# A routed layer of 64 experts at the end of an audio tower: eight rounds of eight experts become one written-out sequence

## The reference, cut to what matters

```
scores = sigmoid(x2 @ gate_w.T)                  # 5520 x 64; top 4 of 8 groups, then top 8 experts
xb = zeros(E, CAP, DIM).at[flat_e, pos].set(x_rep, mode='drop')     # E = 64, CAP = 256, DIM = 128
h  = silu(einsum('ecd,edm->ecm', xb, w1)) * einsum('ecd,edm->ecm', xb, w3)   # 64 hidden columns
yb = einsum('ecm,emd->ecd', h, w2)
y  = yb.at[flat_e, pos].get(mode='fill', fill_value=0.0) * w.reshape(-1)[:, None]
out = h3 + y.reshape(T, K, DIM).sum(1)           # h3 is the stream of 5520 rows before this part
```

## Time and profile before

| | |
|---|---|
| median of 3 runs | 2299.24 us (2298.69 to 2302.49) |
| profiled execution, its own time | 2305.26 us |
| its span in the profile | 2303.4 us |
| busy share of PE, DVE, ACT, POOL over the span | 85%, 63%, 37%, 32% |
| last scatter issued, first add issued, last add issued | 2030.12, 2043.60, 2279.72 us |
| closing DMA issued, end of span | 2283.61, 2303.4 us |

### The profile page before, as it was taken

One profiled execution on the slowest core, in us unless ns is written; L12 is line 12 of the kernel. 1 busy time (PEld: TensorE's weight loads), 2 busy tenths in 40 slices (PEclk: granted clock), 3 DMA queues, 4 the chain that ended last, 5 costly groups with the idle time before them and its releaser, 6 DMA issues. The chain is left out here.

```text
span 2303.4 us, 46715 instructions
## 1 busy us (share of the span) xinstructions
PE 1959.6 (85%) x16960; PEld 1579.7 (69%) x16960; DVE 1457.8 (63%) x4386; ACT 863.2 (37%) x2193; POOL 741.2 (32%) x630
## 2 busy tenths in 40 slices
PE   3688999999999999999999999999988887266660
PEld 2677887888788788878887888788776565133440
DVE  4784465677677766776676766666666668344440
ACT  2453454444344434443434443434334341021120
POOL 1000000013132322323232323232325235768885
PEclk9999999999999999999999999999999899577775
DMA  6874744434344333423342424133200001057665
GB/s 213 277 265 135 252 160 146 144 121 130 93 125 126 111 105 109 124 86 115 94 129 68 121 83 127 50 117 93 80 2 10 6 4 25 8 108 126 115 92 72
DMA packets 167588, 251.52 MB, mean 109 GB/s; under 512 B 67379, under 2 KB 123011, under 8 KB 166608
## 3 DMA queue, kind: packets, MB, share of 16 engines
q10 hardware_dynamic: 43672, 153.59, 20.6%
q0 software_dynamic: 56688, 51.20, 10.4%
q1 hardware_dynamic: 67016, 43.91, 7.3%
HBM read 203.09 MB, written 87.40 MB: 126 GB/s over the span
## 5 line engine op out<-in xcount | busy, mean ns | idle before, releaser
L997 PE MATMUL Cb<-seq_hi,ring 128*128 128x174 f16 x4544 | 599.9, 240 | 20.9 <-DVE seq_lo L1669 10.7
L997 PE MATMUL Cb<-seq_lo,ring 128*128 128x174 f16 x2272 | 528.9, 240 | 0.0
L913 POOL DMA_INDIRECT slots_dram<-rows,slot_i x384 | 454.5, 1184 | 121.1 <-issue 121.1
L997 PEld LDWEIGHTS Cb<-seq_hi,ring 128*128 128x128 f16 x4544 | 405.2, 98 | 52.1 <-DVE seq_lo L1669 11.3
L1491 ACT ACTIVATE area_h<-W,nmax 115x345 f32<-115x345 f32 x384 | 210.3, 548 | 578.9 <-DVE nmax L1986 576.7
L997 PE MATMUL W<-area_k,qv 128*115 128x345 f32 (+1 forms) x1536 | 418.4, 462 | 4.1 <-ACT area_h L1491 2.4
L901 POOL TENSOR_TENSOR rstd<-ve,minus_half 115x3 f32<-115x3 f32 x64 | 59.1, 923 | 1103.4 <-DVE ve L1735 556.9
L1986 DVE TENSOR_REDUCE nmax<-W 115x1 f32<-115x345 f32 x384 | 196.7, 513 | 211.6 <-PE W L997 180.2
L997 PEld LDWEIGHTS Cb<-seq_lo,ring 128*128 128x128 f16 x2272 | 222.0, 98 | 16.5 <-issue 1.3
L1170 PEld LDWEIGHTS W<-ident,area_h 115*115 115x115 f32 x1152 | 165.5, 180 | 94.9 <-ACT area_h L1491 41.2
L1905 DVE SCALAR_TENSOR_TENSOR area_h<-area_h,W 128x345 f32<-128x345 f32 x256 | 131.6, 515 | 147.8 <-ACT area_h L1458 117.8
(11 more groups left out here) (243 smaller groups left out, 2883.6 us busy)
## 6 DMA issues: line engine op xcount, KB each, us to landing
ring<-filters_dram ACTq DMA_DIRECT2D x252, 512.0 KB, 3.5
filters_dram<-ring ACTq DMA_DIRECT2D x36, 512.0 KB, 4.5
slots_dram<-in_empty_slots POOLq DMA_DIRECT2D x8, 1544.0 KB, 13.6
area_k<-slots_dram SPq DMA_DIRECT2D x64, 193.0 KB
band<-band_dram SPq DMA_DIRECT2D x64, 189.0 KB, 2.9
slots_dram<-rows,slot_i POOLq DMA_INDIRECT x384
x_win<-in_xpad SPq DMA_DIRECT2D x16, 252.0 KB
qv<-in_wc POOLq DMA_DIRECT2D x2, 1984.0 KB, 10.9
```

Of the source, the lines that this page charges most:

```text
L913: pool.indirect_dma_start(out=slots_d, out_offset=bass.IndirectOffsetOnAxis(ap=slot_i[parity(b)][:, m:m + 1], axis=0), in_=rows[parity(b)] ...
L997: return pe.matmul(o, l, r, start=start, stop=stop)
```

## The change

The four loops on PE, DVE, ACT and SP over rounds 1 to 7, and POOL's over all eight, become Python loops, so every expert's instructions stand in the stream with constant semaphore values and addresses. On PE and DVE there is one sequence of 64 experts with a lag of four from the first one on (`LAG_E = 4`). Round 0 no longer has its own lag of two, and at a round's end the next round's experts follow on at once. Because the sequence isn't emptied, two waits of PE that a round's first experts did not need are now there for all but the first experts of the kernel. The weights of w1 and w3 get tiles of their own that hold two experts each, of the same total size.

```diff
@@ tiles @@
-        e_w13 = [carve(0, 2 * F1) for _ in range(NE)]
+        e_w1 = [carve(0, 2 * F1).rearrange("p (r n) -> p r n", r=2) for _ in range(NE // 2)]
+        e_w3 = [carve(0, 2 * F1).rearrange("p (r n) -> p r n", r=2) for _ in range(NE // 2)]
@@ SP, and alike on ACT from round 1, on POOL from round 0 @@
-            with sp.Fori(1, E1 // NE) as pr:
+            for pr in range(1, E1 // NE):
@@ PE @@
-                if i >= 4:
+                if pr * NE + i >= 4:
                     pe.wait_ge(t_h.h, t_h.at(pr, i - 3))
...
-                if i >= 2:
+                if pr * NE + i >= 2:
                     pe.wait_ge(t_y.h, t_y.at(pr, i - 1))
...
-            experts(0, 2)
-            with pe.Fori(1, E1 // NE) as pr:
-                experts(pr, 4)
+            for g in range(0, E1 + LAG_E, 2):
+                for k in g, g + 1:
+                    if k < E1:
+                        expert_in(k // NE, k % NE)
+                for k in g - LAG_E, g - LAG_E + 1:
+                    if k >= 0:
+                        expert_down(k // NE, k % NE)
+                for k in g, g + 1:
+                    if k < E1:
+                        expert_up(k // NE, k % NE)
@@ DVE @@
-                    w = e_rows[i][:, c, bass.ds(pr * NE + (C + i), 1)]
+                    w = e_rows[i][:, c, C + pr * NE + i:C + pr * NE + i + 1]
...
-            experts(0, 2)
-            with dve.Fori(1, E1 // NE) as pr:
-                experts(pr, 4)
+            for g in range(0, E1 + LAG_E, 2):
+                for k in g - LAG_E, g - LAG_E + 1:
+                    if k >= 0:
+                        expert_y(k // NE, k % NE)
+                for k in g, g + 1:
+                    if k < E1:
+                        if k % NE == 0:
+                            expert.start(k // NE)
+                        expert_h(k // NE, k % NE)
```

More of the change, by code:

```diff
@@ L43 @@
 FILLS = 8
+LAG_E = 4
 NHID = 2 * (E0 + 1)
@@ L825, in load_weights @@
                 e = pr * NE + i
-                sp.dma_start(e_w13[i][:, 0:F1], dram["w1e"][e]).then_inc(t_load[i].h, 16)
-                sp.dma_start(e_w13[i][:, F1:], dram["w3e"][e]).then_inc(t_load[i].h, 16)
+                sp.dma_start(e_w1[i // 2][:, i % 2, :], dram["w1e"][e]).then_inc(t_load[i].h, 16)
+                sp.dma_start(e_w3[i // 2][:, i % 2, :], dram["w3e"][e]).then_inc(t_load[i].h, 16)
                 sp.dma_start(e_w2[i], dram["w2e"][e]).then_inc(t_load[i].h, 16)
@@ L980, in add_rows @@
                         compute_op=ALU.add).then_inc(t_out[i].h, 16)
-            with pool.Fori(0, E1 // NE) as pr:
+            for pr in range(E1 // NE):
                 for i in range(NE):
@@ L1336, in expert_up @@
                 pe.wait_ge(t_xT.h, t_xT.at(pr, i + 1))
-                if i >= 4:
+                if pr * NE + i >= 4:
                     pe.wait_ge(t_h.h, t_h.at(pr, i - 3))
-                mm(up_bank[i % 4][0:F1, 0:CAP], e_w13[i][:, 0:F1], e_xT[i % 2])
-                mm(up_bank[i % 4][0:F1, CAP:], e_w13[i][:, F1:], e_xT[i % 2]).then_inc(t_hps.h, 1)
+                mm(up_bank[i % 4][0:F1, 0:CAP], e_w1[i // 2][:, i % 2, :], e_xT[i % 2])
+                mm(up_bank[i % 4][0:F1, CAP:], e_w3[i // 2][:, i % 2, :], e_xT[i % 2]).then_inc(t_hps.h, 1)
             def expert_down(pr, i):
                 pe.wait_ge(t_h.h, t_h.at(pr, i + 1))
-                if i >= 2:
+                if pr * NE + i >= 2:
                     pe.wait_ge(t_y.h, t_y.at(pr, i - 1))
@@ L1591, in experts @@
                     expert_tanh(pr, i + 1)
-            experts(0)
-            with act.Fori(1, E1 // NE) as pr:
+            for pr in range(E1 // NE):
                 experts(pr)
```

## The result

Over 18 runs each, the changed kernel took 2306.77 us (2302.25 to 2310.29) and the kernel before 2302.16 us (2298.69 to 2305.82). The ratio is 1.0020, with a 95% interval of 1.0013 to 1.0027, so the change costs 4.6 us (3.0 to 6.2). The forecast was +2.6, 2301.8 in a range up to 2305.0: the direction holds, the time lies outside the range. It also lies over 2303.8, the bound from which the prediction counted a time as slower, to which it gave 13%.

The account below looks back on a forecast made before the run. POOL's back-to-back adds, 128 periods of 1.859 us, bound the experts' phase. Only the longer lag moved the time, +2.6 at the first add, all else 0: 2299.24 + 2.6 = 2301.8 us, range 2298.6 to 2305.0.

Parts of the forecast that it names:

- Rounds no longer emptied: At seven round boundaries: PE and DVE overlap more, but POOL has no gap there to fill; worth 0.
- The lag, +2.6: Start of the experts' phase: down(0) stands behind up(2), up(3), in(4), in(5), so POOL's first add comes 2.6 us later.
- the 2.2 of the rival: Experts' start: PE's clock rises only after the work moved ahead of down(0); +2.2 us, 2304.0 in all; 7%.
- The lower end of the step, 2.2: Lag of four at the start: least delay 2.2 us, with DVE's cast 0.5 after down(0) at full clock.
- step 4: DVE at the start: expert 0's cast, due at 2044.49, meets the end of h(3) at 2044.48; taken as 2044.50.
- Loops written out: All engines' loops: POOL gains nothing at turns, and longer code costs no fetches; 0, at most 1 us lost.
- The rival on supply: Later experts: results fall behind POOL if a slot load takes 7 us longer; once gives +7, 2309; 4%.
- the two slower rivals: Clock rising later at the start, 2304.0, 7%; supply of results falling behind POOL, 2309, 4%.
- the rule on loops: Loop turns: a taken branch outside the fetched window must fetch first, so unrolling would win; the prediction took 0 for POOL.

Follow-up runs that it names:

- POOL's in a loop: Changed kernel with only POOL's loop over the eight rounds kept: 2307.71 us, ratio 1.0019 to the kernel before (2303.08 us).
- four sums: Changed kernel adding to four DRAM sums instead of two, the added two not joined: 2395.60 us, ratio 1.0001 to the kernel before (2394.40 us).
- order in loops: Changed kernel's unbroken sequence with lag of four, rounds 1 to 7 kept as hardware loops: 2397.09 us, ratio 1.0009 to the kernel before (2394.40 us).

## Why the prediction was right and where it failed

1. *What bounds the phase.* Right: POOL's adds, at 1.859 us. In all traces the stretch is 236.11 to 236.16 plus the gaps listed, save two in which a few issues took longer (POOL's in a loop 236.21, four sums 236.29).
2. *Rounds no longer emptied, worth 0.* Right. The order in loops has 236.11, as the kernel before has 236.12; DVE only waits longer for landed adds, 112 us in place of 101.
3. *The lag, +2.6.* Right in place, way and size: +2.34 and +2.61 in the two traces of the changed kernel, +2.55 alone. It depends on when PE's clock rises, a few tenths, not the 2.2 of the rival. The lower end of the step, 2.2, was badly reasoned: it let the cast come 0.5 behind down(0), which no row gives, while step 4 itself has the cast held by h(3).
4. *Loops written out, worth 0, at most 1.* This step failed. It asked whether POOL itself would be short of code or relieved of a loop's turn. The turn is indeed worth 0, but the code's packets are DMAs, and I counted them only as the five before, not as what fifteen would do to others. They lengthen the landing of an add. I had said of landings only that DVE waits for them. That POOL waits for landings, with 4.79 us free and landings up to 4.54, I never worked out, though the kernel's description has this wait. The rival on supply looked at a stream with 7 us to spare and passed over the one with 0.25. Measured: 0.94, 1.40, 0.64, 0.09 and 2.31 us of gaps in the five traces with PE's code written out and everything else in place, 1.1 in the mean. Of the 24 packets of 16 KB in these five, 11 made a landing late.
5. *The base.* The forecast stood on 2299.24, the median of three runs; 18 runs give 2302.16. Of the 5.0 us between 2301.8 and 2306.77, 2.9 are this. I had noted that the profiled execution lay 6.0 above the three and took them all the same. My range made room for their lowest run, not for their highest added to the loss. With 2302.16 as its base the forecast would have been 2304.8 with an upper end of 2307.9, and 2306.77 would have lain inside; that would have been luck as far as the packets go, since the upper end was made for a late clock, which no trace shows. Of the two slower rivals neither happened: the loss beyond the lag has a way that I did not name.

The two parts give 2.34 + 0.94 to 2.61 + 1.40, 3.3 to 4.0 us. The closing stretch is 0.26 and 0.16 shorter in the two traces than in the one of before (over all traces it varies by 0.6), so from the last scatter to the end they are 3.0 and 3.9 us longer, inside the measured 3.0 to 6.2. Whether the 0.7 to 1.6 up to 4.6 is chance stays open: no trace has a place for them, and traces of the changed kernel exist of two executions only. That a refill packet and a late add meet in time is read from ten landings of over 4.85 us in the five traces named under 4, each with a 16 KB packet behind its issue; writing PE's stream as a loop, giving POOL more room, or leaving out the loads takes these gaps away, each in one trace. That the loss grows with the number of packets is not shown.

## What to carry to other kernels

Where an engine issues DMAs back to back and waits for one it issued a little earlier, work out the room: the time to its next wait less the landing seen. If that is a few tenths, whatever else moves packets at that time can count; here it was a longer instruction stream on another engine, on top of loads. A longer lag costs time at the pipeline's start, here 2.3 to 2.6 us, and gained nothing where the last stage never starved. And a base of three runs whose spread is as large as the forecast is no base; put its spread into the range.

## What the runs showed of the hardware that I had not expected

A taken branch cost POOL nothing that its rows show: gaps of 0.30 or 0.31 at all seven turns. That doesn't refute the rule on loops that the prediction cited, since no run here shows whether its condition, a target outside the fetched window, was met by POOL's short loop. Writing PE's loop out raised the 16 KB code packets in the adds' stretch from 1 to 5, one per 31 to 45 us in the changed kernel, and single adds then landed 4.86 to 5.84 us behind their issue instead of 3.2 to 4.7, and POOL lost up to 2.3 us by it. The Trainium skill (Runtime: NRT & Kernel Launch, Instruction fetch mechanics) says that the cost of crossing such a block is mostly hidden. Here POOL's adds paid for it; what PE itself paid was not read.
